# Gathers held at once: by table products, by first-block products and by a spread lead that shrinks from 8 steps to 2

## What is computed

```python
q = (x @ Wq + bq).reshape(n_nodes, 8, 16)
k = (x @ Wk + bk).reshape(n_nodes, 8, 16)
v = (x @ Wv + bv).reshape(n_nodes, 8, 16)
scores = sum(q[targets] * k[sources], axis=-1) * scale + (edge_features @ We + be)
max_s = segment_max(scores, targets)
e = exp(scores - max_s[targets])
denom = segment_sum(e, targets) + 1e-10
weighted = (e / denom[targets])[:, :, None] * v[sources]
agg = segment_sum(weighted, targets)
out = layernorm(x + agg @ Wo + bo)
```

## Time and profile before

| | |
|---|---|
| median of 3 runs | 2408.98 us (2404.39 to 2410.76) |
| profiled execution | 2400.68 us |
| its span, first to last instruction | 2398.6 us |
| granted TensorE clock, mean | 0.750 of full speed |
| instructions | 23254 |

### The profile page before, as it was taken

The page is one execution under the profiler, slowest core; times in us unless marked ns, Lnnn a source line. Parts: engine busy times, 40 slices in busy tenths (PEclk is TensorE's granted clock), DMA queues, the critical chain, the costliest instruction groups (busy, mean ns, idle before and its releaser), DMA issues.

```text
span 2398.6 us, 23254 instructions
## 1 busy us (share of the span) xinstructions
PE 1449.8 (60%) x5480; PEld 979.4 (41%) x5480; DVE 1493.1 (62%) x3591; ACT 526.8 (22%) x1868; POOL 1496.5 (62%) x1572
## 2 busy tenths in 40 slices
PE   5454576656575666565655656565756565656566
PEld 4333353434343444343433434343434343434344
DVE  3365676657566666565666657565666666657666
ACT  0121221212122222222221222122222222222211
POOL 4745546666666666666666666666666666666661
PEclk7666777867677767777787777787877677777786
DMA  6643444545455445454545455454555454545440
GB/s 230 194 111 112 111 133 145 143 144 144 134 153 151 134 125 162 124 162 128 159 131 159 126 152 135 143 145 137 150 147 140 140 146 126 162 126 161 125 126 24
DMA packets 123029, 335.73 MB, mean 140 GB/s; under 512 B 47360, under 2 KB 55301, under 8 KB 115853
## 3 DMA queue, kind: packets, MB, share of 16 engines
q0 software_dynamic: 74624, 203.26, 30.1%
q1 hardware_dynamic: 45520, 124.28, 18.7%
q10 hardware_dynamic: 2748, 6.69, 0.7%
HBM read 323.82 MB, written 10.29 MB: 139 GB/s over the span
## 4 chain that ended last, share of the span: by engine, by line
POOL 32%; another core or an unknown queue 21%; issue 19%; PE 17%; DVE 9%; ACT 2%; DMA 1%; ACTq 0%; DVEq 0%
POOL kv_buf L487 32%; PE ps_a L1191 5%; PE ps_q L1156 4%; DVE prod L787 2%; DVE wv L819 2%; PE ps_t L1156 2%; PE ps_e L1168 1%; DVE score L797 1%; PE ps_a L1234 1%; DVE x_first L807 1%; ACT x_first L559 1%; PE ps_s L1213 1%; DMA kv_buf<-kv_table,src_i 1%; PE ps_s L1219 0%
## 5 line engine op out<-in xcount | busy, mean ns | idle before, releaser
L487 POOL DMA_INDIRECT kv_buf<-kv_table,src_i x1536 | 1468.9, 956 | 842.2 <-issue 437.9
L1191 PE MATMUL ps_a<-wv,x_first 128*128 128x272 f32 x1564 | 571.8, 500 | 325.3 <-ACT wv L605 188.5
L1191 PEld LDWEIGHTS ps_a<-wv,x_first 128*128 128x128 f32 x1564 | 362.3, 242 | 497.1 <-issue 212.1
L787 DVE TENSOR_TENSOR prod<-ps_q,kv_buf 128x512 f32<-128x512 f32 x262 | 179.9, 686 | 472.2 <-remote 296.2
L1156 PE MATMUL ps_q<-q_blk,x_first 128*128 128x256 f32 x1046 | 354.7, 472 | 22.6 <-issue 22.6
L797 DVE TENSOR_REDUCE score<-prod 128x32 f32<-128x512 f32 (+1 forms) x392 | 267.3, 682 | 7.9 <-issue 0.2
L819 DVE TENSOR_TENSOR wv<-kv_buf,ps_w 128x512 f32<-128x512 f32 (+1 forms) x392 | 266.0, 678 | 1.6 <-ACT keep L597 0.2
L1156 PEld LDWEIGHTS ps_q<-q_blk,x_first 128*128 128x128 f32 x1046 | 234.6, 239 | 79.1 <-issue 40.7
L787 DVE TENSOR_TENSOR prod<-ps_t,kv_buf 128x512 f32<-128x512 f32 (+1 forms) x130 | 89.1, 685 | 225.8 <-remote 128.4
L559 ACT ACTIVATE x_first<-dst_bc,neg_node 128x256 f32<-128x256 int32 (+1 forms) x392 | 197.0, 503 | 47.8 <-DMA dst_bc<-in_dst_row 30.4
L568 ACT ACTIVATE x_first<-x_first 128x256 f32<-128x256 f32 (+1 forms) x392 | 157.8, 403 | 215.8 <-remote 193.4
(11 more groups left out here) (140 smaller groups left out, 1550.3 us busy)
## 6 DMA issues: line engine op xcount, KB each, us to landing
edge_f<-in_edge_blk SPq DMA_DIRECT2D x55, 1024.0 KB
dst_bc<-in_dst_row SPq DMA_DIRECT2D x108, 448.0 KB
kv_buf<-kv_table,src_i POOLq DMA_INDIRECT x1536
kv_table<-kv_buf ACTq DMA_DIRECT2D x12, 512.0 KB, 2.7
xt_blk<-in_x_t SPq DMA_DIRECT2D x114, 32.0 KB
out<-y_out SPq DMA_DIRECT2D x114, 32.0 KB
kv_buf<-in_x_perm SPq DMA_DIRECT2D x5, 512.0 KB, 4.2
edge_f<-in_edge_blk SPq DMA_DIRECT2D x2, 512.0 KB
```

The costliest lines, as they stand in the source:

```text
L487: pool.indirect_dma_start(kv_buf[:, b % NBUF, t, :], None, kv_table, bass.IndirectOffsetOnAxis(ap=src_i[:, column:column + 1], axis=0)).th ...
L787: dve.tensor_tensor(prod[:, q % 2, 0:n * D].rearrange("p (t d) -> p t d", d=D), ps_q[q % SPREADS][:, 0:n * D].rearrange("p (t d) -> p t d" ...
L1191: one = pe.matmul(sums(b), edge_hots[:, q % EHOT, k * P:(k + 1) * P], wv[:, q % WVBUF, 2 * k:2 * k + 2, :].rearrange("p j w -> p (j w)"), ...
```

## The change

All of it stands on POOL's queue. The gathers of x for block 0 are issued 8 at once, and then 4 at a time, after 2, 8, 14, 20 and 25 table products. Block 1's first step of gathers waits for all 25 table products, its second for 8 first-block products, and its other five for all 14 of them. From block 2 on a step's second gather waits for a spread: the lead is `15 - q // 2` steps, and never under 2; it is 8 for step 14, 5 for step 21, 3 for steps 24 and 25, and 2 from step 26 on. Blocks 2 to 5 so get a wait for `s_byedge`; block 3 keeps the one for its slot (`HELD` falls to 4), blocks 4 and 5 take those of the later blocks. The flag is now looked at ahead of block 2 rather than of block 3.

```diff
-    HELD, AHEAD = 6, 2
+    HELD, AHEAD = 4, 2
...
+        def spreads_ahead_of(q):
+
+            return q - max(AHEAD, 15 - q // 2) + 1
...
             def gather(b):
                 for g, (t0, t1) in enumerate(STEP[b]):
                     q = FIRST[b] + g
+                    if b == 1:
+                        pool.wait_ge(s_pkv, len(HALVES) + min(8 * g, len(FIRST_HALVES)))
                     if NBUF <= b < HELD:
                         pool.wait_ge(s_weighted, steps_over(b - NBUF, t1))
                     for t in range(t0, t1):
                         column = FIRST_TILE[b] + t
                         if b >= HELD and t == t0:
                             pool.wait_ge(s_summed, q - AHEAD - SLOT - LAG)
-                        if b >= HELD and t == t0 + 1:
-                            pool.wait_ge(s_byedge, q - AHEAD + 1)
+                        if b >= 2 and t == t0 + 1:
+                            pool.wait_ge(s_byedge, spreads_ahead_of(q))
...
             for g, (t0, t1) in enumerate(STEP[0]):
+                if g >= 2:
+                    pool.wait_ge(s_pkv, min(len(HALVES), 6 * g - 10))
                 for t in range(t0, t1):
                     pool.indirect_dma_start(
                         x_first[:, t, :], None, x_rows, bass.IndirectOffsetOnAxis(ap=src_i[:, t:t + 1], axis=0)
...
             gather(1)
             pool.wait_ge(s_fartable, 16)
-            gather(2)
             general = is_general(pool)
             with pool.If(general == 0):
-                for b in range(3, NB):
+                for b in range(2, NB):
                     gather(b)
```

More of the change, by code:

```diff
@@ L989, in _ @@
             with dve.Else():
-                for i in (1, 2):
-                    for g in range(GS[i]):
-                        dve.wait_ge(s_kv[i][g], 16 * (STEP[i][g][1] - STEP[i][g][0]))
+                for g in range(GS[1]):
+                    dve.wait_ge(s_kv[1][g], 16 * (STEP[1][g][1] - STEP[1][g][0]))
                 dve.memset(g_base, 0.0)
```

## The result

| | before | changed |
|---|---|---|
| median of 4 runs each | 2406.68 us (2397.52 to 2410.76) | 2344.61 us (2339.8 to 2346.54) |
| ratio | | 0.975, 95% interval 0.9732 to 0.9768 |
| profiled execution, its span | 2400.68, 2398.6 | 2339.80, 2337.6 |
| granted TensorE clock, mean | 0.750 | 0.748 |

The changed kernel is 2.5% faster, 61.0 us from span to span.

A forecast was written before the change was run, and what follows sets the result against it. No engine was full; late semaphore updates during long gather runs were taken as the bound. Terms summed to -44 + 5 = -39; -44 was taken: 2357 us profiled, median about 2365, given as 2361, range 2335 to 2392.

The forecast's parts named there:

- the second rival: The silences come not from the gathers but, say, from DMA traffic: median of 2414 or no change; chance 0.08.
- x's gathers, -18: Table stage: holds on x's gathers break the long run, so the last bias add ends near 39 us, not 57.
- Block 0's products, the flag, step 0 at 74: After the table: products from 39 to 59 us, the flag 3.5 us later, step 0's product at about 74.
- Block 1's gathers, step 5 at 92: Main loop's start: a run of 21 gathers silences others from about 72 to 88; step 5 at 92, -49 so far.
- Block 2's hold: Steps 5 to 14: POOL waits for spreads, then runs some 16 gathers; the added silence gives back 14 us, leaving -35.
- Steps 14 to 21 at POOL's rate, 35 us: Blocks 2 to 3: products follow at 5.0 us a step, step 21 at 164, -44 in all.
- Steps 21 to 63, +5: 42 steps at the steady 5.81 us take 244 us, against 239 before: 5 us lost.
- main line: The sum of the start's terms, -44 + 5 = -39, with the two added silences at full size.
- The steady pace: From step 63 on, both kernels run the same waits at 5.81 us a step, so the difference stays.
- The first (one place only): Rival: the table keeps its pauses and only the burst of 56 gathers shortens, -26, about 2379; chance 0.18.
- The third: Rival: longer leads make longer gather runs in blocks 2 to 5, +55, so slower, median 2415; chance 0.06.

The follow-up runs named there:

- e7: The kernel before with two POOL memsets after every 8 gathers of x and of blocks 1 and 2, on chip 14: 2383.0 us, ratio 0.9898.
- e2: The changed kernel without the holds on x's gathers, on chip 15: 2052.29 us, ratio 1.0042 to the kernel before.
- e6: The kernel before with the holds on x's gathers alone, on chip 14: 2397.04 us, ratio 0.997.
- e8: The changed kernel without the holds on x's gathers, third set, on a chip without silences: 2047.99 us, ratio 0.9994 to the kernel before.
- e5: The changed kernel, unaltered, on chip 14: 2347.99 us, ratio 0.9762 to the kernel before.
- e12: The changed kernel with six bare POOL pauses replacing the counts for x and block 1, lead kept, on chip 6: 2073.32 us, ratio 1.0121 to the kernel before.

## Why the prediction was right, and what it mis-sized

- **What bounds the kernel.** Right in what is late and beside what: the updates, during long runs. That the gathers have no part in it was the second rival; e7 rules it out where updates are late, since pauses of POOL alone end the silences. But the reading was of one chip. On three others the kernel before takes 15% less time and no update is late beside runs of up to 604 gathers (e2), which nothing in the trace of before told. One reading of rows was too neat: the silences don't last until POOL stops. In the run of x the adds at 20.70 and 29.79 came through while POOL went on the earlier trace rows, in the run of 56 the product at 124.58 did, and the next one, of step 4 at 135.16, came 0.8 us behind that run's end. The rows show three silences that end 2.6 to 3.3 us behind a run, not four.
- **x's gathers, -18.** Measured 39.20 + 0.42 against some 57.2: -18. The first pause came at 17.8, POOL stood until 21.97, as worked out. By itself it is worth 9 us, not 18 (e6), since block 1's run moves up with it. That the next hold, standing behind it, saved the rest in the sum is argued: the kernel without x's holds (e8) ran only on a chip without silences.
- **Block 0's products, the flag, step 0 at 74.** The flag came at 65.06 and not at 63, step 0 at 76.32.
- **Block 1's gathers, step 5 at 92.** It came at 93.14. The run was 25 gathers and not 21, as its second four were still being issued when the last five steps were let go. Its silence was shorter than I said, 7.07 us of VectorE's idle time ahead of 89.24, and not from 72 on.
- **Block 2's hold, a term that was mis-sized.** Forecast: 16 gathers, a silence of 10 to 14 us, steps 5 to 14 in 37 us and step 14 at 129. Measured: 12 gathers (93.02 to 107.7), for step 17's second gather stopped POOL and not step 18's, a silence of 5.68 us, steps 5 to 14 in 28.0 us and step 14 at 121.15. In the repeat (e5) they took 30.2 us, with the same 12 gathers; as step 5 came only at 97.61 there, step 14 came at 127.78.
- **Steps 14 to 21 at POOL's rate, 35 us: the second mis-sized term.** They took 147.80 - 121.15 = 26.7 us (27.0 in e5), 3.8 a step, which is VectorE's own work. The last gather of step 20 was issued by 131, ahead of VectorE, and POOL's waits for the lead, 1.79 to 2.48 us each, cut its runs to 12, 8 and 12, beside which VectorE waits no longer than 1.90 us. I had counted those waits as a cost to POOL only. And I had taken the 44 us of before as a pace of 6.3 a step, where one row, timeline of VectorE, kernel before, has 16.75 us of it as a silence, beside a run of 24 gathers from 159.99 to 190.14:

```profile
193.91 0.69 DVE L787 TENSOR_TENSOR prod<-ps_t,kv_buf 128x512 f32<-128x512 f32 x1 [16.75 <-remote]
```

  44.0 - 16.75 is 27.3: without that silence the steps before went at the same pace as now.
- **Steps 21 to 63, +5: the third mis-sized term.** 383.87 - 147.80 = 236 us against 239 before: -3, and not +5. Step 63 came at 383.87 and not near 408, 24 us early, 16 of them at step 21 and 8 from here.
- **How 24 us became 17.** The profiled execution took 2339.80 us where 2357 was forecast. The forecast took -44 where its main line summed to -39, which made up 5 of the 24; 2 more went behind step 63 (63.3 us sooner there, 61.0 at the end). So the number is nearer than the terms are, and that part is luck.
- **The steady pace** is unchanged, 5.81, as said.
- **The rivals.** The first (one place only) is shut out by the trace after. The third is real as a mechanism: e7 shows it at 88.4 us for 7 steps, where POOL waits for slots only.

What the change leaves: in the steady loop VectorE still falls silent about once a block in both kernels, 8.35 us up to 486.84 before and 8.47 up to 424.37 in the changed kernel, each beside a run of 16 gathers. There the pace is 5.81 us a step against 5.04 in e2, which over 322 steps is 248 us, four times the gain of this change; how much of it is the silences' isn't known. No run here tried to cut these runs.

What stays open: how the gain divides between block 1's holds and the lead on a chip with silences, and whether another shape of the lead, or pauses for counts, would do better there. The kernels for it (e8 to e12) ran on chips of the other kind. Why updates are late on one kind of chip and not on the other isn't settled; no run here varies what could make it so.

## What to carry to other kernels

Read idle time that ends with a late update against what POOL does just then: if it begins ten or more gathers into an unbroken run and ends within 4 us behind the run (some of it can end earlier), cut the run, with a pause that costs POOL nothing it needs; a wait for a count that is a few steps behind is one, and a wait that is always satisfied is none. Judge such a change over the whole start, since a hold only moves the run behind it forward. And measure the kernel before on more than one chip: here the gain is 2.5% where updates come late, and where they don't, variants of the same change are between no change and 0.4% slower, and those with bare pauses 1.2 to 1.9% slower.

## What was not expected of the hardware

- The same kernel takes 2406 us on one chip and 2045 to 2049 on three others, at 956 ns a gather and 1493 us of VectorE's work on both. What differs is the late updates and what follows from them, and also the mean granted clock, 0.75 against 0.80: the matmul that sums by node takes 504 ns on average in the changed kernel and 469 in e2. How much of the 15% is the clock's isn't parted from the silences by any run.
- A gather beside a VectorE operation on two operands in SBUF can take longer, where I had written that no row shows such a lock. The timeline of the changed kernel has:

```profile
56.37 1.76 DVE L758 TENSOR_TENSOR edge_f<-edge_f 128x1564 f32<-128x1564 int32 x1
56.51 2.45 POOL L493 DMA_INDIRECT kv_buf<-kv_table,src_i  x1 [0.30 <-issue]
...
62.26 1.72 DVE L766 TENSOR_TENSOR rel<-rel,base_bc 128x1512 f32<-128x1512 int32 x1
63.02 1.78 POOL L493 DMA_INDIRECT kv_buf<-kv_table,src_i  x1 [0.30 <-issue]
```

  The gather of 0.95 us took 2.45 and 1.78, and ended 0.8 us after VectorE's. The trace of before has the same pair (2.73 us at 72.04, 1.79 at 78.83), so what I had written was wrong of those rows too; and e2, on a chip without silences, has 1.84 and 1.79, so this alone doesn't make updates late. The Trainium skill, "SBUF — State Buffer", Who interferes with whom, says that a VectorE instruction with two SBUF inputs contends with a GpSimd instruction that reads SBUF; the trace agrees in these two places. The page's other sentence, that PE and ACT never wait on anyone, is about ports and tells nothing of the late updates, which hold up ScalarE as well: of the 215.8 us that it idles ahead of L568 in the kernel before, 193.4 end with "remote".
- The silence's start, which is VectorE's last work ahead of it, isn't a fixed time after the run's: 13 to 14 us in many runs of 16 and 20, but 17 us in the run from 159.99 before, 29 us in that from 52.76 here and 36 us in that from 62.05 before. The last two are those in which gathers were so held up; whether that is the reason wasn't tried.
